# Moving the second group's statistics, three scalings and a weight copy at the end of a graph layer

## The reference

```python
h = relu(layernorm(x)); x = x + L0(h)   # softmax attention with adj added to the scores
h = relu(layernorm(x)); x = x + L1(h)   # "second layer"
h = relu(layernorm(x)); x = x + L2(h)   # (adj != 0) @ (h @ W + b) / degree
h = relu(layernorm(x)); x = x + L3(h)   # masked softmax of (h W) U (h W)^T, times adj
```

```python
e    = where(adj != 0, exp(-leaky_relu(s_left[:, None] + s_right[None, :])), 0)
x_a  = (e / (e.sum(1) + 1e-5)) @ (h @ W_sa)
x_b  = adj @ (h @ W_gcnb) + b_gcnb
out  = sigmoid(gate_a * x_a + gate_b * x_b)
```

## Time and profile before

| | |
|---|---|
| median of three runs | 396.99 us |
| profiled execution | 396.94 us |
| its span, first to last instruction | 395.2 us |
| PE busy | 383.2 us (97%) |
| DVE busy | 336.9 us (85%) |
| ACT busy | 251.7 us (64%) |
| POOL busy | 121.9 us (31%) |
| mean granted clock of PE | 0.993 |

### The profile page before, as it was taken

How to read it: one execution, slowest core, us unless ns; L and a number is a source line. 1 busy time by engine, 2 the same in 40 slices (tenths; PEclk the granted TensorE clock), 3 DMA queues, 4 the chain that set the end, 5 groups by cost and what they waited for, 6 DMA issues and landing times. The chain is left out here.

```text
span 395.2 us, 7759 instructions
## 1 busy us (share of the span) xinstructions
PE 383.2 (97%) x2647; PEld 354.4 (90%) x2647; DVE 336.9 (85%) x770; ACT 251.7 (64%) x531; POOL 121.9 (31%) x130
## 2 busy tenths in 40 slices
PE   8999999999999999999999999999999999989895
PEld 6888888999899899999999989998887898989894
DVE  5899899999984957999999989765887898799893
ACT  3553699888895658785787893245332576267772
POOL 1281000001010424223061011061010499379973
PEclk9999999999999999999999999999999999999988
DMA  7995000000000001000000000000000000010011
GB/s 233 375 380 189 0 2 1 2 0 2 0 2 0 2 1 55 2 2 0 3 2 0 3 0 2 2 1 0 2 2 0 2 1 2 0 55 1 2 54 37
DMA packets 10319, 13.99 MB, mean 35 GB/s; under 512 B 660, under 2 KB 7208, under 8 KB 10280
## 3 DMA queue, kind: packets, MB, share of 16 engines
q1 hardware_dynamic: 9736, 12.96, 9.6%
q10 hardware_dynamic: 544, 0.52, 0.4%
HBM read 12.10 MB, written 1.39 MB: 34 GB/s over the span
## 5 line engine op out<-in xcount | busy, mean ns | idle before, releaser
L1637 PE MATMUL ps<-v_hi,p_hi 128*128 128x258 f32 (+3 forms) x242 | 64.1, 295 | 0.3 <-DVE x_sb L1016 0.2
L402 POOL TENSOR_TENSOR mr_all<-mr_all,mhalf 128x4 f32<-128x4 f32 (+1 forms) x12 | 13.5, 1121 | 162.0 <-DVE mr_all L911 162.0
L1638 PE MATMUL ps<-v_lo,p_hi 128*128 128x258 f32 (+3 forms) x242 | 61.0, 282 | 0.0
L1637 PEld LDWEIGHTS ps<-v_hi,p_hi 128*128 128x128 f32 (+3 forms) x242 | 44.7, 185 | 2.1 <-issue 0.9
L1638 PEld LDWEIGHTS ps<-v_lo,p_hi 128*128 128x128 f32 (+3 forms) x242 | 44.8, 185 | 0.5
L1642 PE MATMUL ps<-v_hi,p_lo 128*128 128x258 f32 (+3 forms) x242 | 40.0, 283 | 1.1 <-DVE p_lo L1192 1.1
L998 DVE TENSOR_TENSOR s_sb<-s_sb,ps 128x512 f32<-128x512 f32 (+3 forms) x63 | 38.5, 612 | 1.3 <-PE ps L1624 1.2
L443 POOL TENSOR_TENSOR mid_lo<-adjT_sb,mid_hi 128x512 fp32r<-128x512 f32 (+2 forms) x16 | 22.5, 1406 | 48.5 <-ACT mid_hi L684 48.5
L1642 PEld LDWEIGHTS ps<-v_hi,p_lo 128*128 128x128 f32 (+3 forms) x242 | 32.5, 185 | 1.6 <-DVE p_lo L1192 1.6
L1928 PE MATMUL ps<-big_hi,p_lo 128*128 128x256 f32 (+3 forms) x121 | 32.2, 296 | 0.8 <-ACT p_lo L867 0.6
L1637 PE MATMUL ps<-big_hi,mid_hi 128*128 128x258 f32 (+3 forms) x121 | 31.8, 294 | 0.0
(11 more groups left out here) (249 smaller groups left out, 1217.9 us busy)
## 6 DMA issues: line engine op xcount, KB each, us to landing
adjT_sb<-in_adjT_dram SPq DMA_DIRECT2D x1, 2816.0 KB, 16.6
adjT_sb<-in_adjT_dram SPq DMA_DIRECT2D x3, 768.0 KB, 9.6
adjT_sb<-in_adjT_dram SPq DMA_DIRECT2D x1, 1815.0 KB, 21.5
out_dram<-x_sb SPq DMA_DIRECT2D x10, 128.0 KB
x_sb<-in_x_dram SPq DMA_DIRECT2D x2, 256.0 KB, 3.7
x_sb<-in_x_dram SPq DMA_DIRECT2D x1, 512.0 KB, 4.3
adjT_sb<-in_adjT_dram SPq DMA_DIRECT2D x1, 512.0 KB, 11.9
rows_sb<-in_rows_dram SPq DMA_DIRECT2D x1, 385.0 KB, 11.6
```

Of the source, the lines that this page charges most:

```text
L1637: pe.matmul(out_ap, left_[0][0:k, n % RING, mine], right_[0][0:k, j, 0:cols_], start=(j == 0), stop=False)
L1638: pe.matmul(out_ap, left_[0][0:k, n % RING, mine], right_[1][0:k, j, 0:cols_], start=False, stop=False)
```

## The change

The change moves instructions within the lists of three engines; none is added or removed.

- DVE: `stats` of blocks 4 and 5 go from step 33 to the end of step 36, those of blocks 6 and 7 from step 34 to the end of step 37. `aggr` of blocks 4 to 7, with the two scalings of the constants, go from steps 34 and 35 to step 38, behind `h2_lo(2)` and ahead of `mask_2(5)`. The first group's stay where they were.
- ACT: `scale_b(2)` goes from step 36 to step 38, behind `exp1(32)` and ahead of `z2(4)`. The copy to `gram` goes from step 36 to the end of step 38, behind `h2_hi(4)`.
- PE: the second product of weights goes from behind `aggregate_a(30)` to behind `aggregate_a(32)`, the last of the layer.

```diff
 # ACT
-                    if k == NB * gi + 14:
+                    if k == NB * gi + (16 if gi == 2 else 14):
                         scale_b(gi)
 ...
                 if 38 <= k < NT + LEAD:
                     z2(k - 34)
                     h2_hi(k - 34)
-                if k == 36:
+                if k == 38:
                     act.wait_ge(uw_mm, 1)
                     act.activation(gram[:, :, :], ps[:, 3, :].rearrange("p (c n) -> p c n", c=C),
 # DVE
-                    if step in (1, 2):
-                        stats(b0 + 2 * step - 2, 2)
-                        stats(b0 + 2 * step - 1, 2)
-                    if step in (2, 3):
-                        aggr(b0 + 2 * step - 4, 2)
-                        aggr(b0 + 2 * step - 3, 2)
+                    if gi == 0 and step in (1, 2):
+                        stats(2 * step - 2, 2)
+                        stats(2 * step - 1, 2)
+                    if gi == 0 and step in (2, 3):
+                        aggr(2 * step - 4, 2)
+                        aggr(2 * step - 3, 2)
 ...
                 if 36 <= k < NT + LEAD:
                     h2_lo(k - 36)
+                if 36 <= k < 38:
+                    stats(2 * k - 68, 2)
+                    stats(2 * k - 67, 2)
+                if k == 38:
+                    for b in blocks(1):
+                        aggr(b, 2)
                 if 38 <= k < NT + LEAD:
                     mask_2(k - 33)
 # PE
-                if k == 38:
+                if k == 40:
                     pe.wait_ge(uw_set, 1)
                     weight_product(3, w3T_sb, gram).then_inc(gram_mm, 1)
```

## The result

Six runs of the changed kernel took 400.56 us (median, 400.31 to 401.3), against 397.09 for the kernel before: ratio 1.0089, interval 1.0077 to 1.0101. It is 3.5 us slower; 398.5 was forecast, with a range from 397.3 to 400.1. The profiled execution took 401.3 us with a span of 399.4.

What follows compares the result with a forecast made beforehand. PE was taken as the bound, busy 383.2 of 395.2 us; its 1.61 us gain was outweighed by waiting for the late copy, third layer 1.5 us later: 396.94 + 1.5 = 398.4, median 398.5 us, range 397.3 to 400.1.

Steps and rivals of the forecast that it cites:

- Part 1: DVE's later statistics: both PE waits at tiles 28 and 29 go, up to 1.61 us gained; constants come 2.30 us later.
- Part 2: ACT's scalings and copy: a new 1.1 us wait ahead of z2(4); copy to gram starts at 233.3, ends at 233.87 us.
- Part 3: PE's second product of weights waits for the copy, starts at 233.95 us, takes 1.62 us; third layer 1.5 us later.
- The queue's delay at the third layer: Third layer's first product on PE starts 1.5 us later because the product of weights waits for ACT's late copy.
- It reached the end whole: From the third layer to the end: nothing absorbs PE's delay, so the whole 1.5 us is carried.
- the sum: Whole kernel: 396.94 + 1.5 = 398.4 us profiled, median 398.5 us; chance 0.58.
- the one on the clock: PE's wait of 2 us, 231.9 to 233.9: forecast has no clock fall; rival with a fall 400.0 us, chance 0.13.
- The price of that fall: Clock fall at PE's 2 us wait, as long as that at 375.8: 3.4 x (1 - 0.12/0.22) = 1.5 us.
- The price of the fall at 375.8 us: Half clock from about 375.8 to 379.2 us: its absence was valued at 1.5 us.
- the case of 397.0 us for a vanished fall: Rival: the fall at 375.8 us stays away once everything before is shifted, 398.5 - 1.5 = 397.0 us; chance 0.07.
- The rival of ACT's queue alone: Constants ready when ACT asks, copy ends at 232.77 us, stage 0.4 us later: 397.4 us; chance 0.12.

Runs made afterwards that it cites:

- the second trace: Trace of the changed kernel run again unedited, profiled execution 399.08 us with the clock up at that wait; this rerun's median 399.69 us, ratio 1.0071.
- the wait in the kernel before: Kernel before with only ACT's copy to gram moved from step 36 to the end of step 38, behind h2_hi(4): 401.48 us, ratio 1.0108.
- 16 products of filling: Changed kernel with 16 further products, read by nobody, in PE's list ahead of the wait for the copy to gram: 398.86 us, ratio 1.0045.
- 4 products: Changed kernel with 4 further unread products in PE's list ahead of the wait for the copy to gram: 398.96 us, ratio 1.0051.
- 8 of them: Changed kernel with 8 further unread products in PE's list ahead of the wait for the copy to gram: 399.09 us, ratio 1.0046.
- the constants at step 37: Changed kernel with the second group's four aggr and scalings one step earlier on DVE, end of step 37: 398.76 us, ratio 1.0056.

## Why the prediction was wrong

*Part 1 held.* Both waits for line 1192 at tiles 28 and 29 went. The trace of after runs 0.24 us ahead of that of before, the common offset, which is added to its times here. The instruction behind the scalings was forecast at 230.53 us and came at 230.62 (230.38 in the row). POOL took 1.65 us from the start of the power to the end of the product, forecast 1.52.

*Part 2 held.* ACT's wait ahead of `z2(4)` was forecast with 1.1 us and is 1.11; the copy's start was forecast at 233.3 and is 233.47.

*Part 3 held but for 0.2 us.* The product's start was forecast at 233.95 and is 234.10 (234.11 in the second trace, whose offset is 0.01). The queue's delay at the third layer was forecast as 1.5 us and is 1.67. It reached the end whole, as forecast: the three runs below the gap took 398.6 to 399.1 us, 0.1 to 0.6 over the forecast 398.5. In the profiled one of these 0.4 us came on top in the last layer (1.72 to 2.12 in the table), a term that the sum does not have.

*The step that failed is the one on the clock.* The sum puts the clock's fall at nothing; the fall was named as a rival, with its place and the wait of 2 us, and given a chance of 0.13. Nine of 12 runs lie in the slower group, and the trace from it has the fall. The chance was kept small because the wait of 1.21 us at 350.62 had not brought the clock down, and that row could not bear it. Taking each run above 400 us for one with a fall, the experiments have none in ten at waits of 0 and 0.97 us, one in five at 1.49, two in six at 1.71, nine in 12 at 1.98, and all four at 2.62 us. A wait longer than any near it in the trace lay outside what its rows could tell.

*The price of that fall* was close for the length that it was taken for: 1.5 us for 3.4 us at the lower clock, and the wait in the kernel before has such a fall, at 1.7 us. The fall in the profiled run of after lasted 6.8 us and cost 2.7: the product of weights took 1.6 us more (3.22 against 1.64), and the first ten products of the third layer 1.1 us more. Over the runs of after the two groups differ by 1.6 us, so most falls seem to be cheaper than the profiled one. The measured median is 2.1 us over the forecast; 1.6 of them are this difference, and the rest is what the runs below the gap have too (398.98 against 398.5).

*How far off it came out was in part luck.* The first six runs all lie in the slower group. The six of the same kernel run again have a median of 399.69 us, which is inside the stated range, with the same step missing. On which chip the first six ran isn't on record; the second six, on one chip, fall into both groups by themselves.

*The price of the fall at 375.8 us was too high.* The prediction valued its absence at 1.5 us. Two traces show why that is wrong. With 16 products of filling the clock stays up in the last layer until 395.7 us; with 4 it is at the lower level for 3.4 us from 348.2 and for 6.8 us from 375.5. PE's waits for DVE's low parts in the last layer (total, number, longest), first with 16 and then with 4 products:

```profile
PE ps L1943 <- DVE w_lo L1432: 2.5, 4, 1.2
```
```profile
PE ps L1943 <- DVE w_lo L1432: 0.3, 1, 0.3
```

DVE sets the pace at these places, and a slower PE mostly spends the time that it would have waited. Runs of the kernel before with a mean clock of 0.997 to 0.999 and of 0.991 to 0.993 can't be told apart (both 397.1 us), and those of 0.985 or 0.986 take 397.4. So the case of 397.0 us for a vanished fall had nothing to rest on.

*The rival of ACT's queue alone* would have been 397.4 us. No run shows it by itself; with the constants in time but PE's old waits kept it was 398.1.

## What to carry to other kernels

When an instruction with a wait is put late in a full queue, look at what stands behind it in the same list and who waits for that: here a copy that had nothing to do with the late constants was carried along, and putting it ahead of the waiting one turned 3.5 us of loss into 0.4 us of gain. Price a new wait of the matrix engine with the clock, and when the wait is longer than any that the trace shows, take the trace's shorter waits as no evidence that the clock will stay. Value a slower clock by what the engine would have done with the time: the full price where it sets the pace, little where another engine does (0.4 to 0.8 us here for 10.2 us in the last layer).

## What the runs showed of the hardware

The clock's fall is not a fixed property of a program: one and the same kernel, with the same wait within 0.01 us, has a trace with it and a trace without. Short filling products that nobody reads kept the clock up at that place, and 8 of them (PE's longest standstill then is 0.97 us) did as well as 16, in five runs each.

A long wait isn't needed for a fall either. In the trace of the changed kernel run again the clock fell at about 348.6 us, for 3.4 us, and PE had no wait over 0.21 us in the 112 us before:

```profile
348.00:352.00 4.00, 4.00 (x19) 0.57 0.39 131
```

So the experiments show that a long wait at 232 us makes the fall there likely; they don't show what makes the clock fall elsewhere.

POOL's product of 128 by 4 elements took 0.20 us when DVE stood idle (at 232.00 us in the kernel after, DVE's last instruction before having started at 231.46 with 0.41 us) and 0.86 us when it began while DVE was at work (231.28 us with the constants at step 37). Not every work of DVE's stretches it: in the kernel before, the same product took 0.20 us at 112.42 us, while DVE ran an instruction with one of its two inputs in PSUM (112.33 us, 0.42 us), and 0.24 us at 229.68, where DVE's last instruction ended at 229.86. The Trainium skill (SBUF - State Buffer, "Who interferes with whom") tells of a pair of SBUF ports that GpSimd shares with VectorE as an exclusive lock. By that rule, the traces agree: the short one at 232.00 us came with DVE idle, and starting POOL some 0.6 us earlier into DVE's work brought `z2(4)` only 0.14 us (with each trace's offset).
